# Routed experts moved into the tiles' block: reused buffers, an early norm, and the shared output taken as a difference

## The chip, the cores and the metric

The kernel runs on one core of a Trainium2 chip. The metric is the device time of one execution in microseconds; a run is compared by the median of several executions.

## The reference, cut to what matters

`x` has 128 entries of 32 rows of 512. Three layers are each added to `x`: a block with self and cross attention, a causal attention with 16 heads, and a feed-forward layer with experts. The last one is what the change touches:

```python
x = x + ffn(layernorm(x), ...)
sh = ln(silu(x @ sw1.T + sb1) * (x @ sw2.T + sb2)) * s_ln_g + s_ln_b
shared_out = sh @ sw3.T + sb3
x_moe = x[index_b, index_t]
top1_idx = argmax(sigmoid(x_moe @ eg_w.T + eg_b) + exp_bias)
shared_w, expert_w = softmax([sigmoid(shared gate), score of top1])
final = shared_out.at[index_b, index_t].set(shared_out * shared_w + expert_out * expert_w)
```

Only rows named by the indices go through the 8 experts (two 512 to 256 products, silu, a norm, 256 to 512). The indices in use name rows of one tile alone.

## The kernel before, in words

The rows are cut into 32 tiles of 128 rows (4 entries each). A setup block brings the weights into the form needed, counts from the indices which tiles hold routed rows, and writes to `redo` the number of such tiles and then their numbers; `sel` marks the routed rows. The tiles are laid out in reverse, so that the one tile with routed rows is the last, number 31.

The **tile block** (L408 to L1005) is a pipeline unrolled by `run_pipeline` (L93). In step n each engine does, in the order of its list in `ORDER` (L68 to L88), the named pieces of tiles n, n-1, n-2 and n-3 (the number before the name is the lag). Every engine has its own list, and pieces wait for each other by semaphores. Buffers come in three slots, tile modulo 3. SyncE's own list (near L482) is load_x, load_ctx_t, store, load_ctx_n; it executes its waits and issues DMAs strictly in that order. `store` waits for x2 (input of the last layer, written by VectorE in `project_out`, L795) and stores it to scratch (L476), then waits for the output and stores it (L478). The last pieces of a tile are head_mix (TensorE, L979), project_out, x2_norm, ffn_in (L805), silu and z_norm (VectorE, L649), turn_z (TensorE L849; ScalarE; GpSimd's remainder L503) and ffn_out with its low part ffn_out_l (TensorE L868, L877). Every tile's output, routed or not, is written here with the full shared branch.

The **expert block** (L1008 to L1266) follows, with buffers of its own. Each engine reads the number of tiles from `redo` (L1058) and runs a loop over them; here the loop runs once. SyncE reloads x2 (L1070), then the weights w12, w3, wg of the shared branch and the gate (L1075), small rows (L1077), the biases eb12 (L1079), and per expert `ew12` (1 MB) and `ew3` (0.5 MB) (L1081, L1082). VectorE norms x2 (L1151 to L1173). TensorE turns it (L1237) and makes the product with w12 and the gate's logits (L1224). The shared branch is then done again for this tile: bias, silu (ScalarE L1111), z, moments, gamma and beta, turning, product with w3 (L1244), bias (L1181), plus x2 (L1182). From the gate's scores VectorE picks the expert of each row and its share (L1188 to L1203). For each of the 8 experts: product of all 128 rows (L1224), bias (L1159), silu, z (L1165), moments, the power -0.5 on GpSimd (L1103), gamma (L1210), beta (L1211), times the share, zero for rows of other experts (L1212), turning (L1230), ScalarE's copy (L1115), and the product with ew3, summed in one PSUM bank over all experts (L1264). The last VectorE operation adds this sum (L1215), the output is stored (L1086), and x2 of a next tile, if any or not, is loaded (L1089, issued at L1070).

## Time and profile before

| | us |
|---|---|
| median of 3 runs | 1605.82 |
| the runs | 1604.28, 1605.82, 1607.65 |
| the profiled execution | 1604.27 |
| its span, first to last instruction | 1602.4 |

Busy shares of the span: TensorE 90%, VectorE 67%, ScalarE 36%, GpSimd 27%. TensorE's mean granted clock is 0.966 of full speed. A share is an average over stages: in the middle TensorE is busy nearly all the time, in the last 120 us it is not. In the views PE is TensorE's matmul, PEld its weight load, DVE VectorE, ACT ScalarE, POOL GpSimd, SPq SyncE's queue of DMA issues; brackets give the idle time ahead of an instruction and what ended it.

### The profile page before, as it was taken

What the parts mean: (1) busy time and instruction counts of PE and PEld (TensorE: products, weight loads), DVE (VectorE), ACT (ScalarE), POOL (GpSimd) and SP (SyncE); (2) the same over time, 40 slices, a digit from 0 to 9 for tenths busy, and PEclk for the clock granted to TensorE, in tenths of its full rate; (3) what the DMA queues carried; (4) which work ended last, traced back from release to release, by engine and by line L of the source; (5) the groups of instructions that cost most, each with busy time, mean ns of one, the idle gap of its engine ahead of it and who ended that gap; (6) DMA issues with size and microseconds to landing.
All of it is one profiled execution on the core that took longest, in us unless ns stands there. A gap on an engine that the chain in (4) does not pass through costs nothing. (4 is left out here: it accounts for less than half of the span.)

```text
span 1602.4 us, 31867 instructions
## 1 busy us (share of the span) xinstructions
PE 1440.1 (90%) x13467; PEld 894.3 (56%) x13467; DVE 1073.4 (67%) x2158; ACT 572.6 (36%) x1000; POOL 438.1 (27%) x466
## 2 busy tenths in 40 slices
PE   7178999999999999999999999999999999996486
PEld 3055656666665666666656666665665666653132
DVE  4726777767777777777777777777777777775244
ACT  1412444344333433443444344333433443332110
POOL 0012333233333233323333233333322323322000
PEclk9589999999999999999999999999999999998589
DMA  9143333323322333333333323333333333300180
GB/s 366 75 176 119 133 130 120 104 107 130 126 106 107 132 133 133 133 133 132 133 130 122 104 108 126 124 106 114 127 133 133 133 133 133 126 15 14 65 369 13
DMA packets 35341, 202.36 MB, mean 126 GB/s; under 512 B 4856, under 2 KB 5752, under 8 KB 24448
## 3 DMA queue, kind: packets, MB, share of 16 engines
q1 hardware_dynamic: 35200, 200.34, 34.0%
q8 instruction: 106, 1.74, 0.4%
q14 instruction: 35, 0.29, 0.1%
HBM read 183.29 MB, written 17.04 MB: 125 GB/s over the span
## 5 line engine op out<-in xcount | busy, mean ns | idle before, releaser
L503 POOL TENSOR_TENSOR act_l<-act_t,act_h 128x512 f16<-128x512 f32 x192 | 217.6, 1133 | 398.5 <-ACT act_t L535 398.5
L494 POOL TENSOR_TENSOR rstd<-var,mhalf 128x1 f32<-128x1 f32 x224 | 170.5, 761 | 562.1 <-DVE var L638 562.1
L527 ACT ACTIVATE act_h<-ps_t,scale 128x512 f16<-128x512 f32 (+1 forms) x160 | 103.6, 647 | 200.8 <-PE ps_t L849 200.7
L849 PE MATMUL ps_t<-ident,rows 128*128 128x128 f32 x512 | 82.9, 285 | 45.6 <-DVE rows L642 42.9
L857 PE MATMUL ps_a<-wproj,act_t 128*128 128x512 f32 x256 | 119.3, 610 | 0.7 <-ACT act_t L597 0.7
L857 PE MATMUL ps_a<-wcv,act_t 128*128 128x512 f32 x256 | 115.3, 593 | 0.2 <-ACT act_t L541 0.2
L636 DVE BATCH_NORM_STATS2 stats<-rows 128x6 f32<-128x512 f32 x160 | 111.1, 695 | 5.5
L550 ACT ACTIVATE p_n<-rows,ntop 128x128 f32<-128x128 f32 x32 | 12.9, 402 | 269.0 <-DVE ntop L673 269.0
L535 ACT ACTIVATE act_t<-ps_t,scale 128x512 f32<-128x512 f32 (+1 forms) x160 | 103.0, 644 | 0.0
L868 PE MATMUL ps_a<-w_parts,act_h 128*128 128x512 f16 x384 | 95.9, 387 | 2.1 <-ACT act_h L527 2.1
L649 DVE SCALAR_TENSOR_TENSOR rows<-rows,rstd,beta 128x512 f32<-128x512 f32 x96 | 72.7, 757 | 33.9 <-POOL rstd L494 33.9
L849 PEld LDWEIGHTS ps_t<-ident,rows 128*128 128x128 f32 x512 | 56.1, 142 | 70.0 <-DVE rows L642 66.9
L789 DVE STREAM_TRANSPOSE pbd<-rows 32x512 f32<-32x512 f32 x128 | 89.9, 703 | 4.1
L527 ACT ACTIVATE act_h<-ps_a,scale 128x512 f16<-128x512 f32 x32 | 22.0, 687 | 191.5 <-PE ps_a L849 191.5
L857 PEld LDWEIGHTS ps_a<-wproj,act_t 128*128 128x128 f32 x256 | 50.1, 197 | 64.0 <-issue 55.7
L857 PEld LDWEIGHTS ps_a<-wcv,act_t 128*128 128x128 f32 x256 | 48.5, 190 | 51.0 <-issue 45.9
L645 DVE SCALAR_TENSOR_TENSOR rows<-rows,mv,gamma 128x512 f32<-128x512 f32 x96 | 71.9, 749 | 0.0
L891 PEld LDWEIGHTS ps_a<-act_h,wqk 128*128 128x128 f16 x1024 | 61.3, 99 | 18.9 <-issue 17.7
L509 POOL TENSOR_TENSOR rows<-rows,decay 128x512 f32<-128x512 f32 x32 | 40.7, 1272 | 113.9 <-ACT rows L593 113.9
L541 ACT COPY act_t<-ps_t 128x512 f32<-128x512 f32 x32 | 18.7, 585 | 137.3 <-PE ps_t L849 137.3
L683 DVE SCALAR_TENSOR_TENSOR rows<-ps_t,inv,rows 128x512 f32<-128x512 f32 x32 | 24.0, 751 | 64.2 <-PE ps_t L924 34.7
L891 PEld LDWEIGHTS ps_a<-act_h,wattn 128*128 128x128 f16 x1024 | 58.0, 98 | 13.8 <-ACT act_h L527 13.3
(234 smaller groups left out, 2917.6 us busy)
## 6 DMA issues: line engine op xcount, KB each, us to landing
ctx_t<-in_ctx_t SPq DMA_DIRECT2D x32, 2056.0 KB, 8.4
ctx_n<-in_ctx_n SPq DMA_DIRECT2D x32, 2048.0 KB
x_in<-in_x SPq DMA_DIRECT2D x32, 256.0 KB, 9.4
ctx_last<-in_ctx_last SPq DMA_DIRECT2D x32, 256.0 KB
x_scratch<-rows SPq DMA_DIRECT2D x32, 256.0 KB, 8.8
out<-rows SPq DMA_DIRECT2D x32, 256.0 KB, 2.2
ew<-in_ew SPq DMA_DIRECT2D x8, 1024.0 KB, 19.3
ew<-in_ew SPq DMA_DIRECT2D x8, 512.0 KB, 20.1
```

The lines of the kernel that those rows point to most:

```text
L494: nc.gpsimd.tensor_tensor(rstd[s][:], var[s][:], mhalf[:], ALU.pow).then_inc(rstd_ready[s], 1)
L503: nc.gpsimd.tensor_tensor(act_l[s][:, chunks], act_t[s][:, chunks], act_h[s][:, chunks], ALU.subtract).then_inc(act_l_ready[s], 1)
L527: nc.scalar.activation(act_h[s][:, 0:width // P].rearrange("p c r -> p (c r)"), bank[s][:, 0:width], ACT.Copy, scale=scale[:, k:k + 1]).th ...
L535: nc.scalar.activation(act_t[s][:, 0:width // P].rearrange("p c r -> p (c r)"), bank[s][:, 0:width], ACT.Copy, scale=scale[:, k:k + 1]).th ...
L636: chain(nc.vector.bn_stats(stats[s][:], rows))
L645: return nc.vector.scalar_tensor_tensor(out, rows, mv[s][:, 0:1], g, ALU.subtract, ALU.mult)
L649: return nc.vector.scalar_tensor_tensor(out, out, rstd[s][:], b, ALU.mult, ALU.add)
L789: nc.vector.transpose(pbd[rows, :, g, :], by_head(rows1[s][rows, :])).then_inc(pbd_ready[s], 1)
L849: mm = nc.tensor.transpose(out[s][:, c * P:(c + 1) * P], rows[s][:, lo + c * P:lo + (c + 1) * P], ident[:])
L857: mm = nc.tensor.matmul(out, left[:, c, :], w[:, c, :], start=(c == 0), stop=(c == C - 1))
L868: nc.tensor.matmul(bank[s][:], act_h[s][:, c, :], w[:, part, c, lo:lo + D], start=(c == 0 and part == 0), stop=False, skip_group_check=True)
L891: nc.tensor.matmul(bank[s][:, m * P:(m + 1) * P], w[:, part, c, lo + m * P:lo + (m + 1) * P], act_h[s][:, c, :], start=(m == 0 and c == 0 ...
```

## The change

The separate expert block goes away. Its pieces run inside the tile block.

- **Loads.** When tile 31 has used a weight for the last time, SyncE loads expert weights over it: `early_experts` (lag 1) puts ew12 of the 8 experts into wqk, wv, wcqk, ctx_t, ctx_n and wcv, the first two ew3 into w1, and the small rows into gamma, beta and b1. `late_experts` (lag 2) puts the biases into kbd and pbd and the other six ew3 into wattn. Each waits for the piece of tile 31 that used the buffer.
- **x2 early.** `first_x2` loads x2 behind its store, in front of the last output's store. `first_rows` norms it (VectorE, behind z_norm), turns it and makes the gate's logits (TensorE, behind ffn_out_l of tile 31).
- **Shared branch.** It isn't computed again. The stored output is read back as `old`; `old - x2` is the shared output, and `old + (shared_w - 1) * (old - x2)` for routed rows replaces it.
- **Loop.** The next expert's product stands between the turning of z and the product with ew3; the bias of the next expert stands behind z; the gamma step stands ahead of the wait for the power. The next tile's rows are loaded at the third expert and normed and turned at the sixth, also when there is no next tile.
- **Tile count.** Each engine reads it ahead of the pipeline.

The diff, cut to its core:

```diff
--- before.py
+++ after.py
+        (3, "first_rows"), (1, "context_mix"), (2, "head_scores"), (2, "project_v"), (1, "turn_w"), (0, "turn_xn"),
...
+        (0, "context_scores"), (2, "silu"), (2, "z_norm"), (2, "first_rows")],
...
+    "act": [(3, "ffn_in"), (1, "context_scores"), (3, "turn_z"), (3, "turn_z_t"), (3, "first_rows"), (1, "turn_pc"),
...
+        (1, "out_norm"), (1, "turn_x1n"), (2, "silu"), (2, "first_rows")],
...
+            ew12 = [wide(wqk), wide(wv), wide(wcqk), all_ctx_t[:, 0:WIDE], all_ctx_t[:, WIDE:2 * WIDE],
+                    all_ctx_n[:, 0:WIDE], all_ctx_n[:, WIDE:2 * WIDE], wcv[:].rearrange("p c d -> p (c d)")]
...
+            ew3 = [wide(w1)[:, HC * D * e:HC * D * (e + 1)] for e in (0, 1)]
+            ew3 += [wide(wattn)[:, HC * D * e:HC * D * (e + 1)] for e in range(NE - 2)]
...
+            eb12 = [(all_kbd, all_pbd)[e // 4][:, 2 * H * (e % 4):2 * H * (e % 4 + 1)] for e in range(NE)]
...
+            x2, e_xn, e_xn_t = x_in[s_a], rows1[s_a], act_t[s_a]
+            o, old = flat_rows(q_t[s_a]), v_n[s_a]
+            u, gate = [x_in[s_b], rows1[s_b]], [p_n[s_b][:, 0:H], p_t[s_b][:, 0:H]]
+            z, z_t, diff = p_n[s_a][:, 0:H], p_t[s_a][:, 0:H].rearrange("p (c r) -> p c r", c=HC), flat_rows(act_t[s_b])
+            ps_u, ps_sum, ps_rows, ps_z, ps_gate = (ps_a[s_b], ps_a[s_a]), ps_v, ps_t[s_a], ps_t[s_b], ps_e
...
+                def early_experts(s, r, tile):
+                    if tile == LAST:
+                        sp.wait_ge(q_done[s], 3 * r + 2)
+                        sp.wait_ge(v_done[s], 3 * r + 1)
+                        for e in (0, 1, 2):
+                            load_expert(e)
+                        sp.wait_ge(scored[s], 3 * r + 2)
+                        for e in (3, 4):
+                            load_expert(e)
+                        sp.wait_ge(v_done[s], 3 * r + 2)
+                        for e in (5, 6):
+                            load_expert(e)
+                        sp.wait_ge(rows_done[s], 6 * r + 2)
+                        load_expert(7)
+                        sp.wait_ge(rows_done[s], 6 * r + 3)
+                        for e in (0, 1):
+                            load_expert_out(e)
+                        sp.wait_ge(x_used[s], r + 2)
+                        for dst, name in ((sel_g, "sel_g"), (sel_b, "sel_b"), (bg, "bg"), (ebias, "ebias"),
+                                          (falling, "falling")):
+                            sp.dma_start(dst, a[name].partition_broadcast(P)).then_inc(small_loaded, 16)
+                        sp.dma_start(wg, a["wg"]).then_inc(small_loaded, 16)
+                        sp.dma_start(eb3, a["eb3"]).then_inc(small_loaded, 16)
...
+                def late_experts(s, r, tile):
+                    if tile == LAST:
+                        sp.wait_ge(scored[s], 3 * r + 3)
+                        for e in range(NE):
+                            if e == 4:
+                                sp.wait_ge(y_done[s], r + 1)
+                            sp.dma_start(eb12[e], a["eb12"][e].partition_broadcast(P)).then_inc(bias_loaded, 16)
+                        sp.wait_ge(v_done[s], 3 * r + 3)
+                        for e in range(2, NE):
+                            load_expert_out(e)
+
...
+                    sp.dma_start(x2[:], a["x2"][bass.ds(tile_of(sp, i), 1)].rearrange("a p d -> (a p) d")
+                                 ).then_inc(e_x2_loaded, 16)
+
+                def load_old(i):
+                    sp.dma_start(old[:], a["out"][bass.ds(tile_of(sp, i), 1)].rearrange("a p d -> (a p) d")
+                                 ).then_inc(e_old_loaded, 16)
+                def first_x2(s, r, tile):
+                    if tile == LAST:
+                        for q in SLOTS:
+                            sp.wait_ge(x2_stored[q], 16 * (1 + len(range(q, TILES, SLOTN))))
+                        load_x2(0)
...
+                count = tiles_to_do(sp)
...
+                run_pipeline([(0, "load_x"), (0, "load_ctx_t"), (3, "store_x2"), (3, "first_x2"), (3, "store"),
+                              (0, "load_ctx_n"), (1, "early_experts"), (2, "late_experts")],
...
+                load_old(0)
+                with sp.Fori(0, count) as i:
+                    tile = tile_of(sp, i)
+                    sp.wait_ge(e_x2_used, i + 1)
+                    sp.sem_inc(stats_seen, 1)
+                    load_x2(i + 1)
+                    load_old(i + 1)
+                    sp.wait_ge(e_out_ready, i + 1)
+                    sp.sem_inc(stats_seen, 1)
...
+                    sp.dma_start(a["out"][bass.ds(tile, 1)].rearrange("a p d -> (a p) d"), o).then_inc(e_out_stored, 16)
+                    sp.wait_ge(e_out_stored, 16 * i + 16)
...
+                def first_rows(s, r, tile):
+                    if tile == LAST:
+                        pool.wait_ge(e_var_ready, 1)
+                        nc.gpsimd.tensor_tensor(e_rstd[:], e_var[:], mhalf[:], ALU.pow).then_inc(e_rstd_ready, 1)
...
+                with act.Fori(0, count) as i:
+                    gated(i, 0)
+                    act.wait_ge(logits_ready, i + 1)
+                    nc.scalar.activation(scores[:], logits[:], ACT.Sigmoid).then_inc(scores_ready, 1)
...
+                    for k in range(NE):
+                        act.wait_ge(e_z_turned, NE * i + k + 1)
+                        nc.scalar.copy(z_t.rearrange("p c r -> p (c r)"), ps_z[:, 0:H]).then_inc(e_z_t_ready, 1)
+                        if k + 1 < NE:
+                            gated(i, k + 1)
+                        if k == NEXT_ROWS + 1:
+                            act.wait_ge(xn_turned, i + 2)
+                            nc.scalar.copy(flat_rows(e_xn_t), ps_rows[:]).then_inc(xn_t_ready, 1)
...
+                        dve.wait_ge(e_x2_loaded, 16)
+                        expert_moments(step, x2[:])
...
+                        dve.wait_ge(e_rstd_ready, 1)
+                        nc.vector.tensor_scalar(e_xn[:], x2[:], e_mv[:, 0:1], e_rstd[:], ALU.subtract, ALU.mult
+                                                ).then_inc(xn_ready, 1)
...
+                    biased(0)
+                    dve.wait_ge(logits_done, i + 1)
+                    nc.vector.tensor_tensor(logits[:], ps_gate[:, 0:1 + NE], bg, ALU.add).then_inc(logits_ready, 1)
+                    dve.wait_ge(scores_ready, i + 1)
...
+                    for k in range(NE):
+                        dve.wait_ge(e_gate_ready, NE * i + k + 1)
+                        if k:
+                            dve.wait_ge(e_z_turned, NE * i + k)
+                        step(nc.vector.tensor_tensor(z, gate[k % 2], u[k % 2][:, H:], ALU.mult))
+                        expert_moments(step, z)
+                        step(nc.vector.scalar_tensor_tensor(z, z, e_mv[:, 0:1], sel_g, ALU.subtract, ALU.mult))
+                        dve.wait_ge(e_rstd_ready, (1 + NE) * i + k + 2 + (k > NEXT_ROWS))
+                        step(nc.vector.scalar_tensor_tensor(z, z, e_rstd[:], sel_b, ALU.mult, ALU.add))
+                        nc.vector.tensor_scalar(z, z, pick[:, 3, k:k + 1], None, ALU.mult).then_inc(e_z_ready, 1)
+                        if k + 1 < NE:
+                            biased(k + 1)
+                        if k == 2:
+                            dve.wait_ge(e_old_loaded, 16 * i + 16)
+                            step(nc.vector.tensor_tensor(diff, old[:], x2[:], ALU.subtract))
+                            nc.vector.scalar_tensor_tensor(o, diff, one[:, 7:8], old[:], ALU.mult, ALU.add
+                                                           ).then_inc(e_x2_used, 1)
+                            dve.wait_ge(e_x2_used, i + 1)
+                        if k == NEXT_ROWS:
+                            dve.wait_ge(e_x2_loaded, 16 * i + 32)
+                            expert_moments(step, x2[:])
+                            dve.wait_ge(e_rstd_ready, (1 + NE) * i + k + 3)
+                            nc.vector.tensor_scalar(e_xn[:], x2[:], e_mv[:, 0:1], e_rstd[:], ALU.subtract, ALU.mult
+                                                    ).then_inc(xn_ready, 1)
+                    assert steps[0] == E_STEPS, steps[0]
+                    dve.wait_ge(e_sum_done, i + 1)
                     pe.wait_ge(y_ready[s], r + 1)
...
+                def first_rows(s, r, tile):
+                    if tile == LAST:
+                        turn_expert_rows(1)
+                        pe.wait_ge(small_loaded, 16 * 7)
+                        gate_logits(1)
...
+                for q in range(4):
+                    pe.wait_ge(ew_loaded[q], EW_COUNTS[q])
+                with pe.Fori(0, count) as i:
+                    expert_in(0)
+                    expert_in(1)
+                    pe.wait_ge(coef_ready, i + 1)
...
+                    for k in range(NE):
+                        pe.wait_ge(e_z_ready, NE * i + k + 1)
+                        for c in range(HC):
+                            mm = nc.tensor.transpose(ps_z[:, c * P:(c + 1) * P], z[:, c * P:(c + 1) * P], ident[:])
+                        mm.then_inc(e_z_turned, 1)
+                        if k + 2 < NE:
+                            pe.wait_ge(e_u_ready, NE * i + k + 1)
+                            expert_in(k + 2)
+                        if k == NEXT_ROWS:
+                            turn_expert_rows(i + 2)
+                        pe.wait_ge(e_z_t_ready, NE * i + k + 1)
+                        for c in range(HC):
+                            mm = nc.tensor.matmul(ps_sum[:], z_t[:, c, :], ew3[k][:, c, :], start=False,
+                                                  stop=(k == NE - 1 and c == HC - 1), skip_group_check=True)
+                        if k == NE - 1:
+                            mm.then_inc(e_sum_done, 1)
+                        if k == NEXT_ROWS + 1:
+                            gate_logits(i + 2)
...
-        w12 = sb(fs, "w12", [P, C, 2 * H])
-        w3 = sb(fs, "w3", [P, HC, D])
-        ew12 = sb(fs, "ew12", [P, NE, C, 2 * H])
-        ew3 = sb(fs, "ew3", [P, NE, HC, D])
...
-            load_x2(0)
-            for name, dst in (("w12", w12), ("w3", w3), ("wg", wg)):
-                sp.dma_start(dst[:], a[name]).then_inc(shared_loaded, 16)
...
-            for e in range(NE):
-                sp.dma_start(ew12[:, e], a["ew12"][:, e]).then_inc(ew_loaded[EW_PART[e]], 16)
-                sp.dma_start(ew3[:, e], a["ew3"][:, e]).then_inc(ew_loaded[EW_PART[e]], 16)
...
-                biased(0, b12[:])
-                gated(0)
-                step(nc.vector.scalar_tensor_tensor(z[:], z[:], mv[0][:, 0:1], ln_g[:], ALU.subtract, ALU.mult))
-                nc.vector.scalar_tensor_tensor(z[:], z[:], rstd[0][:], ln_b[:], ALU.mult, ALU.add
-                                               ).then_inc(e_z_ready, 1)
-                dve.wait_ge(shared_done, i + 1)
-                step(nc.vector.tensor_tensor(shared[:], ps_shared[:], b3[:], ALU.add))
-                step(nc.vector.tensor_tensor(o[:], shared[:], x2[:], ALU.add))
```

## Rows read from the trace of the kernel before

**Rows 1.** windows: stretch, busy (count) by engine, TensorE clock, DMA share, GB/s

```profile
1432.00:1509.00 77.00, 51.02 (x344) 26.30 (x336) 36.95 (x67) 17.40 (x27) 13.51 (x15) 0.79 0.04 14
...
1505.00:1510.00 5.00, 3.43 (x8) 1.02 (x8) 0.91 (x2) 0.84 (x2) 0.67 (x1) 0.50 0.00 0
...
1535.00:1540.00 5.00, 5.00 (x9) 2.15 (x10) 1.47 (x3) 1.10 (x1) 0.00 (x0) 0.69 1.03 424
...
1540.00:1585.00 45.00, 40.10 (x99) 16.98 (x98) 23.36 (x65) 7.33 (x19) 3.29 (x6) 1.00 0.44 178
```

**Rows 2.** timeline (start, us, instruction), end of the tile pipeline

```profile
1482.61 1.93 PE L979 MATMUL ps_t<-pbd,v_n 128*32 128x128 f32 x32 [5.29 <-DVE pbd L789]
...
1492.20 0.33 SPq L476 DMA_DIRECT2D x_scratch<-rows  x1
...
1504.68 0.48 DVE L649 SCALAR_TENSOR_TENSOR v_n<-v_n,rstd,ln_b 128x256 f32<-128x256 f32 x1 [0.51 <-POOL rstd L494]
...
1508.16 1.06 PE L877 MATMUL ps_a<-w_parts,act_l 128*128 128x512 f16 x2
```

**Rows 3.** the timeline, entry to the expert block, TensorE, VectorE and ScalarE

```profile
1517.76 0.69 DVE L1151 BATCH_NORM_STATS2 stats<-e_x 128x6 f32<-128x512 f32 x1 [7.02 <-DMA e_x<-x_scratch]
...
1519.64 0.55 DVE L1173 TENSOR_SCALAR e_xn<-e_x,mv,rstd 128x512 f32<-128x512 f32 x1 [0.67 <-POOL rstd L1103]
...
1522.24 1.11 PE L1237 MATMUL ps_t<-ident,e_xn 128*128 128x128 f32 x4 [13.02 <-DMA wg<-in_wg]
...
1524.03 5.58 PE L1224 MATMUL ps_a<-w,e_xn_t 128*128 128x512 f32 x8 [0.68 <-ACT e_xn_t L1119]
...
1529.44 0.95 PE L1224 MATMUL ps_t<-wg,e_xn_t 128*128 128x9 f32 x8
...
1529.64 0.69 DVE L1159 TENSOR_TENSOR e_u<-ps_a,b 128x512 f32<-128x512 f32 x1 [9.45 <-PE ps_a L1224]
...
1530.37 0.42 ACT L1111 ACTIVATE e_gate<-e_u 128x256 f32<-128x256 f32 x1 [6.39 <-DVE e_u L1159]
```

**Rows 4.** the timeline, from the shared branch to the first expert's z

```profile
1534.82 1.28 ACT L1123 ACT_TABLE_LOAD   x1
...
1534.85 3.57 PE L1244 MATMUL ps_v<-w,e_z_t 128*128 128x512 f32 x4 [0.46 <-ACT e_z_t L1115]
...
1540.12 0.21 ACT L1123 ACTIVATE scores<-logits 128x9 f32<-128x9 f32 x1 [4.02 <-DVE logits L1185]
...
1542.88 0.23 DVE L1203 TENSOR_SCALAR pick<-pick,one 128x8 f32<-128x8 f32 x1
...
1548.36 0.43 DVE L1165 TENSOR_TENSOR e_z<-e_gate,e_u 128x256 f32<-128x256 f32 x1 [3.78 <-ACT e_gate L1111]
...
1551.10 0.48 DVE L1210 SCALAR_TENSOR_TENSOR e_z<-e_z,mv,sel_g 128x256 f32<-128x256 f32 x1 [0.66 <-POOL rstd L1103]
...
1552.14 0.35 DVE L1212 TENSOR_SCALAR e_z<-e_z,pick 128x256 f32<-128x256 f32 x1
```

**Rows 5.** the timeline, one expert's turn on TensorE in the steady part

```profile
1559.55 1.98 PE L1264 MATMUL ps_a<-ew,e_z_t 128*128 128x512 f32 x4 [0.46 <-ACT e_z_t L1115]
...
1561.37 3.60 PE L1224 MATMUL ps_a<-ew,e_xn_t 128*128 128x512 f32 x8
...
1565.65 1.98 PE L1264 MATMUL ps_a<-ew,e_z_t 128*128 128x512 f32 x4 [0.46 <-ACT e_z_t L1115]
```

**Rows 6.** the timeline, the last instructions of the kernel

```profile
1595.04 0.69 DVE L1215 TENSOR_TENSOR e_o<-ps_a,e_o 128x512 f32<-128x512 f32 x1 [3.23 <-PE ps_a L1264]
...
1595.91 0.37 SPq L1086 DMA_DIRECT2D out<-e_o  x1
...
1598.86 0.35 SPq L1070 DMA_DIRECT2D e_x<-x_scratch  x1
```

**Rows 7.** the chain that ended last, GpSimd's queue entering the expert block

```profile
1513.31 0.50 POOLq L1058
```

**Rows 8.** DMA issues: tile, count, KB of one, median us to landing

```profile
ew<-in_ew SPq DMA_DIRECT2D x8, 1024.0 KB, 19.3
```

394 lines of the change are left out of this document (164 added, 230 removed).

## The prediction

> **What bounds the kernel now.** I read the slices of the page first, then the windows of the end, then the timeline there. The expert block is a second program part behind 32 pipelined tiles, and only one tile has routed rows, so that block runs once. The change leaves tiles 0 to 30 alone, so only the end counts. There the reader is to see three things [rows 1]. While the last tile drains, the DMA engines stand almost idle (4% of their time, 14 GB/s) and so could carry weights. TensorE's granted clock is 0.50 just before the tiles end, which is 1.2 of its two levels of 1.2 and 2.4 GHz, and 0.69 while the shared branch is recomputed. From 1540 on it is 1.00 and TensorE is busy 40.1 of 45 us: there the experts are bound by TensorE, although the transfers run at 424 GB/s until shortly before. So the weights' transfer is mostly hidden already. What costs is the serial head: TensorE ends the last tile at 1509.22 [rows 2]. The normed x2 is ready only at 1520.19, its transposes wait for the gate weights, the first product starts at 1524.03 [rows 3], and the first expert's z is ready at 1552.49 [rows 4]. That is 43.3 us, of which most belongs to a block entry, a reload and the shared branch.
>
> **Part 1, the head.** In the changed kernel the x2 rows are loaded and normed by VectorE directly behind z_norm of tile 31, which ends at 1505.16 [rows 2]. The norming took 2.43 us, from 1517.76 to 1520.19 [rows 3], so it ends near 1507.6. That is before TensorE ends ffn_out_l at 1509.22, and it costs nothing as long as x2 is in place by 1505.2; past that VectorE, GpSimd's remainder for ffn_out_l and TensorE all come late, about one for one. The cover is ffn_out. GpSimd does one more power ahead of the remainder that ffn_out_l needs; I put 0.2 us for that, between 0 and 0.6. Then, step by step from 1509.2:
> Turning the rows and copying them is 1.79 (from the transposes' start to the first product's, 1522.24 to 1524.03 [rows 3]). The gate's eight products took 0.95 behind a product; here they likely meet the low clock, so between 0.95 and 1.9, and I take 1.5. Expert 0's product is eight matmuls of the same form as the 5.58 of [rows 3], which began low and ended high. The bounds are 3.60 at the high clock [rows 5] and 7.1 at the low one (twice the 3.57 that the four matmuls of the shared output took, mostly low [rows 4]). I take 5.6, since TensorE also comes from the low clock here: it ends at 1518.1. Bias add 0.69 and silu 0.42 [rows 3] with their hand-overs: 1519.3. The sigmoid's table load of 1.28 [rows 4] was hidden beneath the shared branch and is now behind the silu, on the path: 1520.6. Scores 0.25, and from them to the shares of the experts 2.78 (1540.33 to 1543.11 [rows 4]): 1523.6. The z of the first expert took 4.13 (1548.36 to 1552.49 [rows 4]). The bias add of the next expert (about 0.6) now comes behind z, and the gamma step (0.52) now lies beside GpSimd's power, so 3.0: z is ready at 1526.6. Against 1552.49 that is **25.9 us less**. Gone are the block entry, w12 and w3 products, the shared z and its three waits. The old output and x2 instead give "diff" by two VectorE operations in the third expert's slack.
>
> **Part 2, the eight experts.** One turn took 6.10 us, 1559.55 to 1565.65 [rows 5]: 8 + 4 matmuls and a pair of transposes, with ScalarE's copy in the open. The new order puts the next expert's product between transposes and copy, so the copy (about 0.5 with its waits) is covered: 5.6. VectorE does not hold this up: two ScalarE operations and the transposes (1.3) plus the z chain of 3.0 make 4.3 behind each turn. The diff pair falls in the remaining 1.3 us and costs nothing; if TensorE were quicker it would be next. Five turns are 28.0. The sixth also turns a next tile's rows, which are never used, about 0.9: 6.5. The seventh has no product left to cover anything, so the z chain binds: 4.3. From the last z to the output is 3.23 of waiting and 0.69 of work [rows 6]. Together 42.7, where the kernel before has 43.24 (1552.49 to 1595.73): **0.5 less**.
>
> **Part 3, the end.** After the store of the output, issued at 1595.91 and landed by 1598.86 [rows 6], the kernel reloads an x2 that nobody uses. The span ends at 1602.4, thus 3.5 us after that issue, and about 2.8 of them are the transfer. The new one does this and the load of the old output earlier, beside the experts: **2.8 less**.
>
> **Part 4, what is added.** All five engines read the number of tiles from memory ahead of the pipeline. Such a read is 0.50 on GpSimd's queue [rows 7], with some steps around it. It stands before the first x load, on the start's path: 0.7 more, between 0 and 1.7. At the end those reads were part of the 43.3 above. After expert 1's product TensorE has nearly nothing to do for about 5 us, as before the shared output, which then took 3.57 for four matmuls against 1.98 at the high clock [rows 4, 5]. So I charge one fall of the clock, 1.6, and 0.7 for a second at the thin seventh turn: 2.3, between 0 and 5. The loads in the tile part move 14 MB into idle DMA time [rows 1] and are charged nothing. SP waits in order: behind the early loads' wait for out_norm of tile 31 stands tile 30's x2 store, which nobody needs before the first reload; behind the late loads' wait for head_mix stands tile 31's x2 store (see the second rival).
>
> **Sum.** 25.9 + 0.5 + 2.8 - 0.2 - 0.7 - 2.3 = 26.0 us less. The profiled run took 1604.27 us, 1.87 more than its span, and becomes 1578.3. The median of the runs shown is 1605.82, 1.55 above it, so the forecast is **1579.8 us**, with 1575 to 1585 from the bounds of this case.
>
> **Rivals.**
> The clock stays high, or comes back earlier: TensorE was busy 3.43 of the 5 us from 1505 [rows 1] and now goes on, where before it stood still until 1522.24 [rows 3]. Then expert 0's product is 3.6, the gate's 0.95, and no fall is paid: 4.8 less, 1575. Against it speaks the 0.50 [rows 1].
> **x2 comes late.** The late loads (half of the biases and six output weights, 4 MB) can start only when head_mix of tile 31 ends at 1484.54 [rows 2]. At 424 GB/s they last till about 1497. Ten issues at 0.33 to 0.37 each [rows 2, 6], or somewhat more, leave SP free before 1492.20, when the x2 store is issued [rows 2] on the same queue; with its landing and the reload at some 2.5 to 3 us each I expect x2 at 1501 to 1503, 2 to 4 us early. But a weight's median from issue to landing is 19.3 us [rows 8]. If the store took that, x2 would come at 1514.3, TensorE would follow 8 to 10 us late: 1589. The Trainium skill (DMA: Bandwidth & Descriptors, on queues, rings and completion order) says that each DMA engine takes the descriptors of one ring in order, which is the mechanism of this rival; no row here shows a small store behind such a backlog.
> **Code is fetched at the loop.** Falling from the unrolled tiles into a loop may stall an engine; before, that lay beneath the waits for data. The nearest row is the last reload, up to 3.5 us for a round trip and the end. If TensorE pays about 3: 1583. The Trainium skill (Runtime: NRT & Kernel Launch, on instruction fetch) says that only a taken branch out of the fetched pages costs such a fetch; a loop run once may take none, and no row decides it.
> **The loads disturb the tiles.** 14 MB beside the last tile's dependent work, a few us: 1583 to 1586. Against it: while 424 GB/s flowed, TensorE was busy 5.00 of 5.00 us [rows 1].
> **Slower than before.** The clock stays at 1.2 GHz through the experts. At twice the time a matmul, a turn of 5.6 becomes about 11; eight experts and the head's products then give back about 38 us, net 12 over: 1618. It decides from the point where the low clock outlasts five turns. For it speaks only the 0.50 ahead of the block; against it, that the same sparser loop ran at 1.00 for 45 us.
> That the change does not move what it says could only be with more than one tile to do; the trace has one pass.
>
> **Chances.** Forecast 0.61, clock high 0.14, x2 late 0.08, code fetch 0.09, disturbed tiles 0.04, clock low 0.04 (a quarter of that near no change, since it may last part of the way). 0.2% (3.2 us) is about what a measurement can tell here. So faster 0.96, same 0.01, slower 0.03. The range that leaves out under two in ten is 1573 to 1588.
>
> **What would show it.** Right: x2's norming ends before TensorE's ffn_out_l; the gate's products start within 2 us of it; first z near 1527, turns of 5.6 us, last output store near 1570; the x2 reload issued before 1500; no wait of TensorE for an expert's weights. Wrong: VectorE or GpSimd waiting for the x2 reload past 1506; TensorE idle at the loop's start with nothing late; the first tile more than 1.7 us later; granted clock under 1 past 1535; a turn still at 6.1.

## The result and the profile after

The changed kernel takes **1578.24 us** (median of 4 runs, 1577.05 to 1579.05) where the kernel before took 1605.05 in the same comparison (4 runs, 1604.19 to 1607.65): a ratio of 0.983 with a 95% interval of 0.9813 to 0.9847, which is 26.8 us or 1.7% faster. The forecast was 1579.8, counted from the earlier median of 1605.82. The profiled execution took 1579.05, its span is 1577.2, and TensorE's mean granted clock in it is 0.965 (0.966 before). Its span is 25.2 us shorter than that of before. The next paragraphs read where these 25.2 come from, in four places.

The first fence is the windows view of the changed kernel: stretch, its length, busy us (count) of PE, PEld, DVE, ACT and POOL, TensorE's granted clock, DMA share, GB/s.

```profile
1432.00:1509.00 77.00, 51.60 (x355) 26.85 (x353) 38.43 (x70) 17.76 (x27) 12.84 (x14) 0.79 0.57 212
...
1515.00:1520.00 5.00, 5.00 (x12) 2.93 (x13) 0.00 (x0) 0.00 (x0) 0.00 (x0) 0.50 0.30 105
...
1530.00:1535.00 5.00, 4.54 (x7) 1.84 (x7) 2.28 (x5) 2.07 (x3) 0.30 (x1) 0.50 0.00 0
...
1540.00:1570.00 30.00, 29.04 (x84) 13.73 (x82) 19.84 (x53) 3.91 (x11) 4.87 (x7) 1.00 0.07 18
```

Against [rows 1]: the drain of the last tile now carries 212 GB/s instead of 14, and the experts' stretch carries 18 instead of 178. The clock is at its low level (0.50) beneath expert 0's product and again at 1530 to 1535, then at its high one to the end. TensorE is busy 29.04 of 30 us in the loop.

The second fence is the timeline of the changed kernel (start, us, instruction, idle before and its cause), from the last tile to the first expert's z. Its tiles have new names, since the expert part uses the tiles' buffers: `x_in` is x2, `rows` its norm, `beta` the gate's weights, `wqk` expert 0's, `p_n` an expert's z.

```profile
1495.93 0.34 SPq L537 DMA_DIRECT2D x_scratch<-rows  x1
...
1506.02 0.36 SPq L585 DMA_DIRECT2D x_in<-x_scratch  x1
...
1508.48 0.48 DVE L831 SCALAR_TENSOR_TENSOR v_n<-v_n,rstd,ln_b 128x256 f32<-128x256 f32 x1 [0.51 <-POOL rstd L635]
1508.88 0.69 DVE L1014 BATCH_NORM_STATS2 stats<-x_in 128x6 f32<-128x512 f32 x1
...
1511.96 1.06 PE L1152 MATMUL ps_a<-w_parts,act_l 128*128 128x512 f16 x2
...
1514.64 1.85 PE L1273 MATMUL ps_e<-beta,act_t 128*128 128x9 f32 x8 [0.77 <-ACT act_t L758]
1516.34 6.22 PE L1305 MATMUL ps_a<-wqk,act_t 128*128 128x512 f32 x8
...
1523.76 1.28 ACT L781 ACT_TABLE_LOAD   x1
...
1530.85 0.35 DVE L1093 TENSOR_SCALAR p_n<-p_n,pick 128x256 f32<-128x256 f32 x1
```

**The tiles** end at 1513.02 (end of ffn_out_l), 3.80 later than the 1509.22 of [rows 2]. **The head**, from there to z at 1531.20, is 18.18 us instead of 43.27 [rows 2, 4]: 25.1 less. The norm of x2 (1508.88) starts directly behind z_norm, with no idle time, but only just: the reload was issued at 1506.02, 10.1 us after the store, and lands late. The row of the DMA issues (count, KB each, median us from issue to landing):

```profile
x_in<-x_scratch SPq DMA_DIRECT2D x2, 256.0 KB, 2.7
```

That puts x2 at about 1508.7 (an estimate from the median of two such loads), 0.2 ahead of its use.

The third fence is the same timeline for the loop and the end.

```profile
1531.26 0.69 PE L1322 MATMUL ps_t<-ident,p_n 128*128 128x128 f32 x2 [0.46 <-DVE p_n L1093]
...
1538.58 0.38 PE L1322 MATMUL ps_t<-ident,p_n 128*128 128x128 f32 x2
...
1542.24 1.88 PE L1331 MATMUL ps_v<-w,p_t 128*128 128x512 f32 x4
...
1547.61 1.88 PE L1331 MATMUL ps_v<-wattn,p_t 128*128 128x512 f32 x4
...
1565.88 0.38 PE L1322 MATMUL ps_t<-ident,p_n 128*128 128x128 f32 x2
...
1570.18 0.44 PE L1322 MATMUL ps_t<-ident,p_n 128*128 128x128 f32 x2 [0.69 <-DVE p_n L1093]
...
1573.11 0.69 DVE L1110 TENSOR_TENSOR q_t<-ps_v,q_t 128x512 f32<-128x512 f32 x1 [2.98 <-PE ps_v L1331]
...
1574.04 0.37 SPq L618 DMA_DIRECT2D out<-q_t  x1
```

**The loop** takes 42.60 from z to the output's end at 1573.80, against 43.24. Its steady turn, from one pair of transposes to the next, is 5.37 (1542.24 to 1547.61 for the same step of it) instead of 6.10 [rows 5], but the first is 7.32. It also holds one more product than the loop of before: there the third expert's product (1547.70, 3.70 us) stood ahead of the first z, here it stands behind it. **The end**, from the output to the last instruction, is 3.40 instead of 6.67: 3.27 less. Together 25.1 + 0.6 + 3.3 - 3.8 = 25.2.

### The profile page after: what moved, and what is told of

It is laid out like the page before. It is cut to its first block, busy times and chain, and to the rows that moved or that the text cites. A ratio compares the mean times of both kernels' runs of the same rounds, so it can differ in the third digit from the quotient of the medians.

```text
span 1577.2 us, 31858 instructions
## 1 busy us (share of the span) xinstructions
PE 1439.5 (91%) x13465; PEld 897.8 (57%) x13465; DVE 1070.7 (68%) x2154; ACT 571.6 (36%) x999; POOL 438.8 (28%) x466
## 4 chain that ended last, share of the span: by engine, by line
PE 45%; DVE 25%; issue 9%; POOL 8%; ACT 7%; DMA 0%; DVEq 0%; SPq 0%; POOLq 0%
POOL rstd L635 8%; PE ps_a L1132 8%; DVE stats L818 7%; PE ps_t L1124 4%; PE ps_a L1166 4%; PE ps_a L1223 4%; PE ps_v L1143 4%; PE ps_t L1143 3%; DVE rows L831 3%; ACT L753 2%; DVE rows L824 2%; PE ps_a L1188 2%; PE ps_t L1254 2%; DVE mv L819 2%; PE ps_a L1178 2%
## 5 line engine op out<-in xcount | busy, mean ns | idle before, releaser
L1166 PE MATMUL ps_t<-act_h,wcqk 128*128 128x128 f16 x1024 | 65.7, 225 | 1.6 <-ACT act_h L679 1.6
```

The source lines that it names most:

```text
L1166: nc.tensor.matmul(bank[s][:, m * P:(m + 1) * P], w[:, part, c, lo + m * P:lo + (m + 1) * P], act_h[s][:, c, :], start=(m == 0 and c == 0 ...
```

## The experiments

Most are the changed kernel with one edit. "x2's rows early" has two, the last joins three, and of the three with a delay one has late reads as well and one is the kernel before. "Before" was run beside each batch (medians 1604.09, 1606.5 and 1606.59), and the ratios are to it. The changed kernel's own ratio, 0.983 (0.9813 to 0.9847), is the one to hold them against. "More" and "less" are differences of medians from 1578.24, although the batches differ; taken by the ratios these differences move towards faster by 0.3 to 1.4 us in the first two batches, and by 0.9 to 3.3 in the third (late output weights and the delays). The intervals of five kernels overlap the changed kernel's: weights at the end, old order, third product, late output weights, and the delay. For these the medians alone prove no difference, and the trace has to carry the reading.

### x2's norm late

The reload of x2 and its norm, turn and gate go back behind the last tile's output.

```diff
-(3, "store_x2"), (3, "first_x2"), (3, "store"),
+(3, "store_x2"), (3, "store"), (3, "first_x2"),
-(2, "z_norm"), (2, "first_rows")]
+(2, "z_norm"), (3, "first_rows")]
-(2, "silu"), (2, "first_rows")]
+(2, "silu"), (3, "first_rows")]
```

> The x2 reload and its norm go back behind the last tile's output; all else stays as changed (1578.2 us). Theory A (the gain is the serial head: entry, reload, norm and shared branch taken off the path): the reload is issued with the last output store near 1514.6, lands 2.9 us later, the norm takes 2.4, so TensorE turns the rows near 1520 where it now does so at 1512.8: 7 us slower, 1585. Theory B (the gain is the transfer of the weights, brought under the tiles): under 1.5 us slower. Theory C (the gain is the new order in the expert loop): no change.

1585.34 (1584.74 to 1585.64), ratio 0.9871 (0.9848 to 0.9895): 7.1 more. Its timeline, SyncE and VectorE:

```profile
1514.66 0.37 SPq L585 DMA_DIRECT2D x_in<-x_scratch  x1
...
1517.34 0.69 DVE L1014 BATCH_NORM_STATS2 stats<-x_in 128x6 f32<-128x512 f32 x1 [4.26 <-DMA x_in<-x_scratch]
```

VectorE waits 4.26 for x2 and TensorE for VectorE: that chain is what the early norm removes. The expectation, 1585, was met.

### All expert weights at the end

The loads of `early_experts` and `late_experts` (weights alone, the small rows stay) are issued behind the pipeline, each expert's product waiting for its own.

```diff
-for e in (0, 1, 2):
-    load_expert(e)
...
 load_old(0)
+for e in range(NE):
+    load_expert_out(e)
+    if e + 2 < NE:
+        load_expert(e + 2)
```

> The 16 expert weight loads (12 MB) are issued behind the last output's landing, as late as before, in order of use and with a wait for each pair; biases and gate rows stay early. Theory A: only the first two weights' landing is on the path, about 6 us from issue near 1517.5 against a first product at 1516.3; later ones arrive at 3.8 us per expert against a turn of 5.4. 5 to 8 us slower, 1583 to 1586. Theory B: 15 us or more slower, 1593 and up. If the early loads had disturbed the last tile, the tile part would end 2 to 3 us earlier here than in the changed kernel.

1584.03 (1582.3 to 1585.64), ratio 0.9864 (0.9839 to 0.9889): 5.8 more, as expected. TensorE's timeline:

```profile
1521.56 2.93 PE L1301 MATMUL ps_a<-wqk,act_t 128*128 128x512 f32 x3 [7.99 <-DMA wv<-in_ew]
```

Expert 0's product waits 7.99 for its weights; the later turns are again 5.37, so after the first the transfer keeps ahead. From the first transposes (77.86) to the end of ffn_out_l (1510.92) the tiles take 1433.06 us; in the kernel of the norm late, which carries the loads, it is 78.51 to 1511.57, the same 1433.06, at about the same clocks: **the 12 MB of expert weights do not disturb the tiles.** The 2 MB of biases and the small rows were early in both.

### The shared branch computed again

A shared branch is put back ahead of the experts: one more pass of product, silu, z, norm, turn and product. It uses expert 0's weights, and its result goes unused.

```diff
+for c in range(C):
+    mm = nc.tensor.matmul(ps_u[0][:], e_xn_t[:, c, :], ew12[0][:, c, :], start=(c == 0), stop=(c == C - 1))
+pe.wait_ge(e_z_ready, (1 + NE) * i + 1)
...
 expert_in(0)
```

> A pass as long as the old shared branch (product, bias, silu, z, norm, turning, product of two chunks, two additions) is put in front of expert 0, on expert 0's weights, its result unused. Theory A: in the kernel before, 14.2 us lay between the start of that product and the start of expert 0's, 0.95 of them the gate's: 13 us slower, 1591. Theories B and C: TensorE's extra matmuls alone, 5 us or less.

1588.98 (1585.57 to 1592.24), ratio 0.9888 (0.9859 to 0.9917): 10.7 more, where 13 were expected. The four runs are two pairs: 1585.57 and 1586.6 at a mean granted clock of 0.969 and 0.966, 1591.37 and 1592.24 at 0.963. In the profiled run, the slowest of them, the first expert's z is turned 12.65 later than the 1531.26 of the changed kernel:

```profile
1543.91 0.69 PE L1351 MATMUL ps_t<-ident,p_n 128*128 128x128 f32 x2 [1.09 <-DVE p_n L1109]
```

By the medians this is the largest single part of the gain, 7 to 14 us from the fastest run to the slowest.

### The loop in its old order

TensorE again makes the next expert's product ahead of the transposes of z.

```diff
-pe.wait_ge(e_z_ready, NE * i + k + 1)
-(transposes)
 if k + 2 < NE:
     pe.wait_ge(e_u_ready, NE * i + k + 1)
     expert_in(k + 2)
+pe.wait_ge(e_z_ready, NE * i + k + 1)
+(transposes)
```

> TensorE's order in a turn as before: the next expert's product ahead of the turning of z, ScalarE's copy in the open again. Theory A: a turn is 5.9 to 6.1 again instead of 5.37, so 3 to 4 us over six turns, but the third expert's product fills TensorE's gap ahead of the first z and the clock may stay high there, which gives back 3 to 5: between 2 us faster and 2 slower. Theory C: 6 us or more slower.

1582.61 (1580.33 to 1584.5), ratio 0.9851 (0.9826 to 0.9875): 4.4 more, and a missed expectation. TensorE's timeline:

```profile
1530.65 5.86 PE L1305 MATMUL ps_a<-wcqk,act_t 128*128 128x512 f32 x8
1536.35 0.38 PE L1325 MATMUL ps_t<-ident,p_n 128*128 128x128 f32 x2
...
1542.45 0.38 PE L1325 MATMUL ps_t<-ident,p_n 128*128 128x128 f32 x2
```

The turn is 6.10 again, as in [rows 5], with ScalarE's copy in the open. I had hoped that the third product would fill the thin stretch ahead of the first z. It did not: it still stands behind the wait for the coefficients, started at 1530.65 and ran at the low clock (5.86 for 8 matmuls instead of 3.60). So the first z, ready at about the same time, is turned at 1536.35 instead of 1531.26, 5.1 later; from there to the last transposes the two kernels are nearly equal (39.29 against 38.92). That is why the new order is worth 4.4 here, although the loop, counted from the first z, gained only 0.6: the order moved one product out of the head.

### The counts read behind the pipeline

```diff
-                count = tiles_to_do(sp)
                 run_pipeline(...)
+                count = tiles_to_do(sp)
```

and so on the four other engines.

> All five engines read the number of tiles behind the pipeline instead of ahead of it. Theory A (the reads and the steps around them stand on the start's path, where the changed kernel's first transposes come 0.9 us later than the kernel before's; at the loop's entry four of the five engines wait for data anyway): the first transposes near 77.5 us, x_scratch of the last tile about 0.9 us earlier, total about 0.9 less than the changed kernel, 1577.3. Theory B (the read does not cost at the start, or costs TensorE the same 0.5 to 0.9 us at the loop's entry, where TensorE follows VectorE's norm of x2 directly): no difference, 1578. Theory C (how the granted clock's levels fall on the first stages decides more than the read): the start is earlier and the tile part's end isn't, or differs by 2 us or more.

1572.06 (5 runs, 1570.77 to 1573.04), ratio 0.9788 (0.9775 to 0.9802): 6.2 less, far more than the read can cost. The timeline of the start, of the changed kernel and then of this one:

```profile
71.38 0.17 DVE L343 CAST redo<-ps_e 1x32 int32<-1x32 f32 x1
73.00 0.33 SPq L520 DMA_DIRECT2D x_in<-in_x  x1
...
78.38 1.11 PE L1124 MATMUL ps_t<-ident,rows 128*128 128x128 f32 x4 [7.11 <-DVE rows L824]
```

```profile
70.60 0.17 DVE L343 CAST redo<-ps_e 1x32 int32<-1x32 f32 x1
71.41 0.33 SPq L520 DMA_DIRECT2D x_in<-in_x  x1
...
76.45 1.12 PE L1124 MATMUL ps_t<-ident,rows 128*128 128x128 f32 x4 [5.96 <-DVE rows L824]
```

From `redo` to the first transposes it is 7.00 with the reads ahead and 5.85 with them behind (5.88 in the kernel before): the reads cost **1.15 us** there. The two profiled runs are 7.45 us apart, and the rest of it lies elsewhere. The setup, the same in both, ends 0.78 earlier. The tiles, from the first transposes to the end of ffn_out_l, take 1432.3 us instead of 1434.6; the difference lies in the fill, the first tiles of the pipeline, as shown below. The edit touches no instruction there. And the head takes 15.3 us to the first z's transposes instead of 18.2, although the reads now stand in it, between the gate and expert 0's product, where they cost TensorE 0.30:

```profile
1511.74 3.67 PE L1305 MATMUL ps_a<-wqk,act_t 128*128 128x512 f32 x8 [0.30 <-issue]
```

Fill and head both differ in the granted clock, which the delay experiments below are about. Whether the place of the reads has a part in it is not shown.

### The third product early

```diff
 expert_in(0)
 expert_in(1)
+pe.wait_ge(e_u_ready, NE * i + 1)
+expert_in(2)
 pe.wait_ge(coef_ready, i + 1)
...
-if k + 2 < NE:
-    pe.wait_ge(e_u_ready, NE * i + k + 1)
-    expert_in(k + 2)
+if k + 3 < NE:
+    pe.wait_ge(e_u_ready, NE * i + k + 2)
+    expert_in(k + 3)
```

> TensorE multiplies the third expert's product ahead of its wait for the coefficients, as soon as VectorE has read the first one's, and expert k+3 in turn k. Theory A (the gap of some 5 us in front of the first z's transposes is what lets the clock fall to 0.50 in 1530 to 1535, and the third product fills most of it): the first turn 5.4 instead of 7.3, one product of 1.9 to 3.6 us less behind it, the window 1530 to 1535 near 1.00; total 2.5 to 4.4 less, near 1575. Theory B (the clock's fall follows from what was done before 1525 and no product in the gap changes it): the window stays at 0.50, the third product takes about 3.6 in the gap, and only its 1.9 us of the turns is won: about 1576.5. Theory C (VectorE's chain of about 4.3 us a turn binds as soon as TensorE is ahead): turns stay near 5.4 for TensorE or become bound by VectorE, total within 1 us of the changed kernel.

1576.43 (1574.76 to 1577.09), ratio 0.9811 (0.9796 to 0.9826): 1.8 less by the medians, with an interval that overlaps the changed kernel's. The trace can be compared directly, since its tiles end (1512.75) and its first z comes (1530.99) nearly as in the changed kernel. TensorE's timeline:

```profile
1525.56 3.60 PE L1305 MATMUL ps_a<-wcqk,act_t 128*128 128x512 f32 x8
...
1530.99 0.44 PE L1324 MATMUL ps_t<-ident,p_n 128*128 128x128 f32 x2 [0.26 <-DVE p_n L1093]
...
1536.84 0.38 PE L1324 MATMUL ps_t<-ident,p_n 128*128 128x128 f32 x2
```

The gap is filled, the granted clock is 1.00 from 1525 on, and the first turn is 5.85 instead of 7.32. From the first z's transposes to the last it is 37.26 us instead of 38.92. Theory A had the clock right and the gain too high: the last two turns, with no product left, are bound by VectorE's chain at 5.15 and 4.36 (5.81 and 4.30 in the changed kernel), so the product moved away from them gives back only 0.6. Theory B's figure, 1576.5, was hit by luck: it went with a clock that stays at 0.50.

### x2's rows early, late output weights behind the reload

VectorE's norm goes ahead of ffn_in, TensorE's turn behind ffn_in_l (ScalarE's and GpSimd's lists are changed to match), and six `ew3` loads move from ahead of x2's store to behind its reload.

```diff
-(2, "silu"), (2, "z_norm"), (2, "first_rows")]
+(1, "x1_norm"), (2, "first_rows"), (2, "ffn_in"), ... (2, "silu"), (2, "z_norm")]
-(3, "first_rows"), (1, "context_mix"), ...
+(2, "ffn_in_l"), (2, "first_rows"),
-(3, "store_x2"), (3, "first_x2"), (3, "store"),
+(3, "store_x2"), (3, "first_x2"), (3, "late_out"), (3, "store"),
```

> The norm, turn and copy of x2's rows move ahead of ffn_in on VectorE, behind ffn_in_l on TensorE, and the six late output weights are issued behind x2's reload instead of ahead of its store. Theory A (x2's store waited behind the weights on the queue, 10.1 us from its issue to the reload's; without them that is 3.0): the reload is issued by 1500, the norm is done before VectorE's ffn_in, TensorE's turn of the rows no longer stands behind ffn_out_l, and the gate starts at its end: 1.8 to 3.3 us less, 1575 to 1576.5. Theory B (x2 still comes late, the norm then holds up ffn_in and with it the whole last tile): the same or up to 5 us slower, 1578 to 1583. Theory C (the output weights now come too late for the loop, which waits for all parts of them): TensorE waits for weights at its loop's start, about 2 us slower.

1573.72 (1572.35 to 1574.12), ratio 0.9796 (0.9781 to 0.9811): 4.5 less, more than the 1.8 to 3.3 of theory A. Its timeline, SyncE and TensorE:

```profile
1495.05 0.34 SPq L537 DMA_DIRECT2D x_scratch<-rows  x1
1498.03 0.36 SPq L588 DMA_DIRECT2D x_in<-x_scratch  x1
...
1505.99 1.03 PE L1276 MATMUL ps_e<-beta,act_t 128*128 128x9 f32 x8 [1.42 <-ACT act_t L761]
...
1511.92 4.51 PE L1308 MATMUL ps_a<-wqk,act_t 128*128 128x512 f32 x8
```

The gate is done before z_norm's transposes, and expert 0's product follows ffn_out_l (end 1512.13) at once; the first z is turned at 1525.13, 13.0 after that end instead of 18.2. The first turn loses 0.9 of it (8.23 instead of 7.32, at a low clock), and the tiles took 1.1 less in this profile. Expert 0's product took 4.51 instead of 6.22, so part of the head's gain is again the clock's.

### Only the late output weights moved

The last line pair of the diff above, alone.

> Only the six late output weights are moved behind x2's reload; all else as in the changed kernel. Theory A (the weights on the queue hold the x2 store up for 7 us, but the norm's slack just covers that: VectorE went from z_norm to the norm with no idle): the reload is issued by 1500 instead of 1506, and the time stays at 1578 within 0.5. Theory B (GpSimd or VectorE did wait for x2 by some tenths, or the weights disturb the last tile): up to 1 us less, 1577 to 1578. Theory C (the loop now waits for output weights): slower by 1 to 2 us.

1576.59 (1572.47 to 1579.02), ratio 0.9814 (0.9799 to 0.9829), overlapping the changed kernel's. Its timeline (the profiled run is the one of 1572.47):

```profile
1492.81 0.34 SPq L537 DMA_DIRECT2D x_scratch<-rows  x1
1495.79 0.36 SPq L588 DMA_DIRECT2D x_in<-x_scratch  x1
...
1505.34 0.48 DVE L834 SCALAR_TENSOR_TENSOR v_n<-v_n,rstd,ln_b 128x256 f32<-128x256 f32 x1 [0.51 <-POOL rstd L638]
1505.74 0.69 DVE L1017 BATCH_NORM_STATS2 stats<-x_in 128x6 f32<-128x512 f32 x1
...
1511.49 1.03 PE L1276 MATMUL ps_e<-beta,act_t 128*128 128x9 f32 x8 [0.77 <-ACT act_t L761]
1512.38 3.68 PE L1308 MATMUL ps_a<-wqk,act_t 128*128 128x512 f32 x8
```

Without weights ahead of it the store lets the reload be issued after 2.98 us instead of 10.1, and VectorE's norm starts against z_norm exactly as before: 0.40 after its start in both. So the late x2 was real and cost nothing; the slack just held. The 1.65 by which the median is lower is within the noise. This run also is the changed kernel's loop and head in another draw of the clock: gate 1.03 and product 3.68 at the high level, where the changed kernel's profiled run had 1.85 and 6.22. From ffn_out_l's end (1509.87) to the first z's transposes (1524.76) it is 14.9 us. The four runs go from 1572.47 at a mean granted clock of 0.970 to 1579.02 at 0.965: 6.5 us between executions of one kernel.

### A delay at the start, three times

VectorE does two operations of 128x512 at the end of the setup whose result nobody reads, in the kernel with late reads, in the changed kernel and in the kernel before.

```diff
 nc.vector.tensor_copy(redo[:, 1:1 + TILES], ps_e[0:1, 4:4 + TILES])
+for n in range(2):
+    nc.vector.tensor_scalar(pause[:, n, :], gamma[:], 1.0, None, ALU.mult)
```

> The counts are read behind the pipeline as in the run before it that gained 6.2, but VectorE does two operations of 128x512 (0.55 each, their result unused) at the end of the setup, so that the pipeline starts as late as with the reads ahead of it. Theory A (the reads cost only their 1.15 us of start; the other 5 us that their move gained came from where the granted clock fell in relation to the work: a dip at 110 to 115 in the fill that was gone, and the high clock from 1510 on under the first expert products): with the start back at its old place the dip is back and most of the 5 us are lost again, 1576 to 1578. Theory B (the reads ahead of the pipeline do harm beyond the start, and the gain belongs to their place): 1.1 more than with the reads late, 1573.2. Theory C (the 6.2 were chance between runs): anything from 1572 to 1578, with no dip and no pattern.

> The changed kernel with the same two idle VectorE operations at the end of the setup: 1.1 us later start, nothing else. Theory A (where the clock falls decides): the total moves by something other than 1.1, either way, between 1575 and 1582, and the windows of the fill (105 to 115) and of the head (1510 to 1530) show which dips moved. Theory B (a delay is a delay): 1579.3.

> The kernel before, with the same two idle VectorE operations at the end of the setup and nothing of the change. Theory A (a start 1.1 us later brings the clock's dip at 110 to 115 into the fill, which the changed kernel has and the kernel before has not): 2 to 4 us slower than the kernel before, with a granted clock near 0.50 in 110 to 115. Theory B (a delay is a delay, the dip belongs to the changed kernel): 1.1 slower, clock 1.00 there.

Reads late and a delay: 1574.16 (1572.86 to 1574.73), ratio 0.9792 (0.9778 to 0.9805), 2.1 more than without the delay, of which 0.8 is the delay itself (6.65 from `redo` to the transposes against 5.85) and 1.1 the tiles (1433.4 against 1432.3). So neither theory's number: a lower clock is back in the fill (0.66 in 105 to 110 us and 0.65 in 110 to 115), but not in the head, where the first z came 15.3 after the tiles as without the delay.

The changed kernel with a delay of 1.08: 1578.65 (1574.07 to 1579.24), ratio 0.9812 (0.9797 to 0.9827), no different from 1578.24, and its profile has 0.50 in the same places of fill and head. Its fastest run, 1574.07, had a mean granted clock of 0.970, the others 0.966 and 0.967. With the delay, moving the reads behind the pipeline gained 4.5 us by the medians (1578.65 to 1574.16, though the intervals of the two ratios overlap), and 6.2 without it, while the trace charges the reads with 1.43 and 1.15 at the start. The start's time alone does not explain that gain, so theory B of the first expectation, harm beyond the start, is not excluded.

The kernel before with a delay of 0.68: 1606.45 (10 runs, 1605.89 to 1609.97) against 1606.59 (15 runs, 1604.25 to 1608.82), ratio 1.0003 (0.9994 to 1.0012): theory A's 2 to 4 us are out, a plain 0.68 (a ratio of 1.0004) is not. Its ten runs all have a mean granted clock of 0.959 to 0.964; of the fifteen without the delay, six have 0.966 or 0.967 and took 1604.25 to 1605.73, nine have 0.962 to 0.964 and took 1605.95 to 1608.82. The windows view shows 110 to 115 us, of the kernel before, the changed kernel, the one with the output weights moved, and the kernel before with the delay, in this order:

```profile
110.00:115.00 5.00, 4.78 (x26) 2.54 (x25) 0.00 (x0) 1.75 (x3) 1.16 (x1) 1.00 0.98 351
```

```profile
110.00:115.00 5.00, 4.25 (x11) 2.74 (x12) 1.15 (x2) 1.85 (x3) 0.84 (x1) 0.50 1.04 381
```

```profile
110.00:115.00 5.00, 4.78 (x20) 2.50 (x21) 0.32 (x1) 1.75 (x3) 1.16 (x1) 1.00 0.96 358
```

```profile
110.00:115.00 5.00, 5.00 (x12) 2.60 (x12) 0.00 (x0) 1.85 (x3) 1.16 (x1) 0.67 0.95 344
```

The last of them has 0.65 in 105 to 110 as well, so the low level, the dip, lies across both windows. From the first transposes to ffn_out_l's end these four took 1431.8, 1434.6, 1432.4 and 1434.3. The timeline shows the dip in one product of the fill, of the kernel before and then of the changed kernel:

```profile
110.81 3.70 PE L857 MATMUL ps_a<-wcv,act_t 128*128 128x512 f32 x8 [0.22 <-ACT act_t L541]
```

```profile
112.54 5.00 PE L1132 MATMUL ps_a<-wcv,act_t 128*128 128x512 f32 x8
```

The same stretch of work, from the start of the 16 matmuls `ps_a<-ctx_n,p_t` ahead of this product to the start of `ps_a<-act_h,wqk` behind it, took 7.66 us in the kernel before, with late reads and with the late output weights moved, and 10.10 in the changed kernel, with late reads and a delay, and in the kernel before with a delay: 2.44 for the dip. Over all the tiles such pairs differ by 1.1 (late reads without and with the delay) to 2.6. The dip comes with and without the change, and the profiled run of before, 1604.27 and near the bottom of its 15 later runs, had been one without it. Held against it, the changed kernel's profiled run, which has the dip, looks some 2 us worse than the change is.

### The three edits together

Reads behind the pipeline, third product early, x2's rows early.

> The three edits together: counts read behind the pipeline, the third product ahead of the coefficients, x2's rows ahead of ffn_in with the late output weights behind the reload. If each gains what it does alone and they add up (0.9 + 3.5 + 2.5): about 1571. If the head's gain is lost because VectorE's chain to the first z binds instead: about 1574. If one of them is a loss alone, this shows less than the better of the others.

**1569.55** (5 runs, 1568.21 to 1570.77), ratio 0.9771 (0.9758 to 0.9784): 8.7 less than the changed kernel and the fastest of the study, by 2.5 over the reads alone. That is 1.5 under the 1571 expected. The first z is turned 13.0 after the tiles (their end is 1510.42), the first turn is 5.85, and the clock is 1.00 from 1515 on:

```profile
1523.44 0.44 PE L1327 MATMUL ps_t<-ident,p_n 128*128 128x128 f32 x2 [0.26 <-DVE p_n L1096]
...
1529.29 0.38 PE L1327 MATMUL ps_t<-ident,p_n 128*128 128x128 f32 x2
```

## Why the prediction was right, and where it was not

The time came out 1.6 below the forecast and the mechanism is the one forecast: the serial head goes away, and the experiments show it. That the sum came so near is in part luck: the tiles' end cost 2.9 more than charged and the head gave 0.8 less, but the loop with the falls of the clock, forecast at 1.8 lost, gained 0.6, and the end gave 0.5 more. That makes 25.2 in the profiled runs against 26.0 forecast, and 26.8 by the medians. Point by point:

- **Head, 25.9 predicted, 25.1 found.** From the tiles' end to z it is 18.2, not 17.4. Expert 0's product took 6.22 instead of 5.6 and the gate 1.85 instead of 1.5, both beneath a clock at 0.50 until about 1521; z took 3.11 instead of 3.0. The table load lay on the path with the 1.28 predicted. The prediction gave the head only as a whole; taken back one at a time, the shared branch is worth 10.7, the early norm 7.1 and the early weights 5.8. They need not add, since x2 and the weights wait beside each other. By the run at the high clock (14.9), some 3 of the 18.2 are the clock's.
- **Loop, 0.5 predicted, 0.6 found, with two errors that cancel.** The turn is 5.37, not 5.6, since the copy's cover saves the whole 0.73; over the five turns counted that is 1.2. The seventh is 4.30 as forecast, the sixth 5.81 instead of 6.5. The first turn, 7.32, takes it back. That one fall of the clock was predicted in the added costs (1.6; 1.95 found, 7.32 less 5.37), so it stands in the 0.6 found and not in the 0.5 predicted; the second (0.7) did not come.
- **End, 2.8 predicted, 3.27 found.** The transfer that nobody waits for is worth a little more than its transfer time.
- **Reads at the start, 0.7 predicted, 1.15 found**, within the bound of 1.7. It is the steadiest number of the study: from `redo` to the transposes eight profiles with the reads ahead and no delay have 6.99 to 7.28, two with them behind 5.84 and 5.85, and with the delay it is 8.08 against 6.65.
- **The tiles' end, 0.9 later predicted (0.7 for the reads, 0.2 for the extra power), 3.80 found.** This is the step that failed, hidden by the others. Its setup ended 0.2 earlier, 1.1 are the reads, and 2.9 lie in the tiles. For the greater part that is the clock's dip in the fill: two profiles of the changed tiles that have nearly the clock of before there take 1432.3 and 1432.4, 0.6 more than before, which leaves 2.2 to 2.3 for the dip. Of the 0.6, 0.4 to 0.5 lie ahead of tile 0's ffn_out_l (107.99 us from the first transposes to the start of its last matmuls before, 108.40 and 108.47 in these two), again in the fill; the cause of the rest is open. The extra power cost nothing: from z_norm's end to ffn_out_l's end it is 4.06 in both kernels (1505.16 to 1509.22, 1508.96 to 1513.02). I compared against one profiled run and took its clock for the kernel's.
- **x2's slack.** "2 to 4 us early" was wrong, and so was the sign "the x2 reload issued before 1500": with the landing at about 1508.7, the 2.7 of such a reload behind 1506.02, and z_norm's end at 1508.96, it was near 0.2. The store's landing, 2.5 to 3 us in the prediction, is 3 with nothing ahead (2.98) and took 10.1 behind the six output weights. The 4 MB at 424 GB/s give 9.9 us, thus 1494.4 and not 1497; in the trace the transfers ran at 404 GB/s until 1502, with the tiles 3.8 later. The rival that x2 comes late (0.08) was therefore nearer than its chance said: by this count a landing 0.2 later would have begun to hold VectorE up. The Trainium skill (DMA: Bandwidth & Descriptors, on queues, rings and completion order) says that a DMA engine takes the descriptors of one ring in order. 10.1 against 2.98 agrees with that; no run separates the order from the bandwidth that the weights took.
- **Rivals that fell.** Disturbed tiles: 1433.06 with and without the expert weights. Code fetched at the loop: TensorE goes from the gate (1514.64, 1.85 us) to the product (1516.34) with no idle. Clock stuck low: 1.00 from 1540 on. The clock-high rival, 1575, did not happen in the changed kernel's four runs, but did in runs of two kernels that are nearly the same: 1572.47, with gate and product at 1.03 and 3.68, and 1574.07.

What stays open: what sets where the granted clock falls in the fill and in the head. It is not the start's time alone (first transposes at 76.87 with a dip in two kernels and at 77.91 in a third, at 76.45, 77.43 and 77.86 without one); nor is it settled why late reads gain 5 us more than their 1.15, and 3 more than their 1.43 with the delay. That this is where the work falls in relation to the clock is argued from the profiles, not shown. Reads late with and without the delay kept the high level in the head, in the profiled run of each; the kernels with early reads showed both.

## What to carry to other kernels

Here the serial head between two pipelined parts was worth more than the transfers around it: start its input's reload and norm in the last tile, and derive what the first part has already stored instead of computing it again. Put a small store that somebody waits for ahead of the bulk loads on its queue, even where the slack just holds. And before a difference of 2 or 3 us between two profiled runs is put down to an edit, compare the granted clock of the same stretch in both, the mean granted clock of every run, and the medians.

## What was not expected of the hardware

- A 256 KB store took 2.98 us from its issue to the issue of the reload that waits for it, and 8.4 to 10.4 us in seven profiles behind six loads of 0.5 MB on the same queue.
- Reading the tile count into a register on five engines ahead of the pipeline cost 1.15 us from the data to the first matmul; on SyncE, the time from `redo` to its first load went from 0.81 to 1.62.
- In the changed kernel TensorE was idle for 4.0 us (1505.0 to 1509.0), and then its clock stood at 0.50 through 12 us of nearly unbroken work (1509 to 1521). With the late output weights moved it was idle for the same 4.0 us (1501.9 to 1505.9) ahead of the same instructions, and its clock was at 1.00 from 1512 to 1520, beginning some 6 us after work began again. In the run with a third product in the 5 us gap ahead of the first z, it stayed at 1.00 through 1530 to 1535, where the changed kernel's was 0.50.
- Four executions of one kernel, the one with the late output weights moved, took 1572.47 to 1579.02 us, with mean granted clocks of 0.970 to 0.965.
